# Eight-column expert masks spread by a matrix product in a fused scan, expert and feed-forward kernel

## The reference

```
tf    = sigmoid(sum(cond, -1))                      # one number for a batch
decay = exp(-exp(w)) * (0.5 + 0.5 * tf)             # channel x batch
a forward and a backward scan of exp(k) * v and of exp(k), with that decay
base  = sigmoid(r) * (num / den);  out = base * (0.8 + 0.2 * tf)
layer 0, experts:
gate  = argmax(x @ Wg.T);  p = softmax(x @ Wg.T)[gate]
h     = x @ A[e].T for all 8 experts, times one_hot(gate)
y     = sum over e of h[e] @ Bw[e].T, times 4 * p
layer 1, feed-forward:
w1, w2 made ternary (sign where |w| >= 0.7 * mean|w|);  gelu(x @ w1.T + b1) @ w2.T + b2
```

## Time and profile before

| | us |
|---|---|
| median of 3 runs | 103.11 |
| lowest and highest | 102.61, 103.37 |
| the profiled execution | 102.21 |
| its span on the core | 100.4 |

### The profile page before, as it was taken

How to read it: one execution, slowest core, us unless ns; L and a number is a source line. 1 busy time by engine, 2 the same in 40 slices (tenths; PEclk the granted TensorE clock), 3 DMA queues, 4 the chain that set the end, 5 groups by cost and what they waited for, 6 DMA issues and landing times. The chain is left out here.

```text
span 100.4 us, 2070 instructions
## 1 busy us (share of the span) xinstructions
PE 89.8 (89%) x633; PEld 80.9 (81%) x633; DVE 86.5 (86%) x203; ACT 79.9 (80%) x144; POOL 66.3 (66%) x90
## 2 busy tenths in 40 slices
PE   3897669989978999999799999999899999799980
PEld 2686549977777888888588888889799999699970
DVE  2479999999999999999999999999999997983330
ACT  4279999999986769999766589997997899976520
POOL 4067679979985697059769897999982967005310
PEclk9999999999999999999999999999999999999999
DMA  1889999700000000000000000000000021100005
GB/s 20 258 262 320 308 245 378 313 3 0 3 0 0 3 0 7 0 0 0 0 3 0 7 0 0 0 0 0 0 0 7 0 104 70 35 0 10 0 0 209
DMA packets 6886, 6.43 MB, mean 64 GB/s; under 512 B 2370, under 2 KB 6492, under 8 KB 6876
## 3 DMA queue, kind: packets, MB, share of 16 engines
q1 hardware_dynamic: 6868, 6.31, 20.1%
q10 hardware_dynamic: 8, 0.00, 0.0%
HBM read 5.26 MB, written 1.05 MB: 63 GB/s over the span
## 5 line engine op out<-in xcount | busy, mean ns | idle before, releaser
L298 POOL TENSOR_TENSOR h_lo<-h,h_hi 128x512 fp32r<-128x512 f32 x9 | 12.3, 1373 | 12.0 <-DVE h_hi L306 7.0
L794 DVE TENSOR_TENSOR_SCAN run<-bank,kv 128x256 f32<-128x256 f32 x32 | 20.0, 670 | 0.1
L1224 PE MATMUL bank<-xin_hi,w1T 128*128 128x256 f32 x64 | 15.8, 287 | 0.9 <-DVE xin_lo L292 0.5
L1156 PE MATMUL bank<-num,AT 128*128 128x256 f32 x64 | 15.5, 384 | 0.7 <-DVE hm L900 0.5
L1258 PE MATMUL bank<-w2T,h_hi 128*128 128x256 f32 x64 | 16.1, 288 | 0.0
L1258 PE MATMUL bank<-w2T,h_lo 128*128 128x256 f32 x64 | 15.6, 281 | 0.0
L611 ACT ACTIVATE h<-bank,bT 128x256 f32<-128x256 f32 x32 | 13.3, 478 | 2.8 <-PE bank L1224 2.6
L1224 PE MATMUL bank<-xin_lo,w1T 128*128 128x256 f32 x64 | 15.2, 278 | 0.0
L1172 PE MATMUL bank<-hm,BT 128*128 128x256 f32 x64 | 14.6, 382 | 0.1
L1224 PEld LDWEIGHTS bank<-xin_hi,w1T 128*128 128x128 f32 x64 | 12.0, 188 | 1.8 <-DVE xin_lo L292 0.8
L1156 PEld LDWEIGHTS bank<-num,AT 128*128 128x128 f32 x64 | 11.6, 190 | 2.2 <-issue 0.9
(11 more groups left out here) (141 smaller groups left out, 216.5 us busy)
## 6 DMA issues: line engine op xcount, KB each, us to landing
w_nat<-in_L_ffn_w_dram SPq DMA_DIRECT2D x2, 1024.0 KB, 8.3
F_nat<-in_fside_BxSxS_dram SPq DMA_DIRECT2D x4, 256.0 KB, 3.5
x_nat<-in_x_dram SPq DMA_DIRECT2D x4, 256.0 KB, 4.9
out_dram<-outb SPq DMA_DIRECT2D x3, 256.0 KB, 2.1
A_nat<-in_L_ffn_A_dram SPq DMA_DIRECT2D x1, 512.0 KB, 5.8
B_nat<-in_L_ffn_Bw_dram SPq DMA_DIRECT2D x2, 256.0 KB, 6.6
out_dram<-outb SPq DMA_DIRECT2D x2, 128.0 KB, 1.9
wv_rows<-in_L_cond_w_dram SPq DMA_DIRECT2D x2, 1.0 KB
```

Source lines behind the costliest of these rows:

```text
L298: eng.tensor_tensor(h_lo[:, b % 2, 2 * j:2 * j + 2], h32[:, b % 2, 2 * j:2 * j + 2], h_hi[:, b % 2, 2 * j:2 * j + 2].bitcast(F32), ALU.sub ...
L794: dve.tensor_tensor_scan(run[:, r, c, q], decay_ps[:, l, c, b:b + 1].broadcast_to([P, T]), kv[:, b, c, q], 0.0, ALU.mult, ALU.add).then_in ...
L1156: mm = pe.matmul(bank[H_BANK + k][:, (m % 2) * T:(m % 2 + 1) * T], AT[:, c, m * P:(m + 1) * P], num_at(0, b)[:, c], start=(c == 0), stop=( ...
L1224: mm = pe.matmul(bank[g_bank[g]][:, (f % 2) * T:(f % 2 + 1) * T], w1T[:, c, f * P:(f + 1) * P], part[:, b % 2, c], start=(c == 0 and part ...
```

## The change

The mask has 8 columns, one for each expert, instead of 128. `transpose_mask` turns it into 8 partitions, a new `copy_hot(b)` (ACT) takes these to SBUF, a new `spread_mask(b)` (PE) multiplies a constant 8x128 matrix `spread` (1 where p // 16 is e) with them, and `copy_mask(b)` takes the product as before. `spread` is made by POOL with a memset and two selects ahead of its first clip. The exponentials of `w` are taken on the four loaded rows, in place, before they are transposed, `decays` reads the transposed rows from PSUM, and `transpose_u`, which writes the same place, waits for both outputs of `decays`. The calls are moved in the lists as the diff shows: `decay_exps` stands ahead of the first key exponential; on PE `warm_up(2)` goes, four transposes of the identity (`fill(4)`) stand between `transpose_mask(0)` and `spread_mask(0)`, `place_residual(1)` and `spread_mask(1)` stand ahead of `expert_in(1, 0)`, `transpose_mask(2)` stands ahead of `expert_in(2, 1)` and `transpose_mask(3)` ahead of `hidden(0, 0)`; on DVE `select_expert(0, 0)` stands ahead of `gate(1)`. The second threshold is computed from the total itself instead of from the first. Three pairs of semaphores are merged, and the reciprocal of the mask has a call of its own.

```
         identb = sb("identb", [P, P], BF16)
-        expert_of = sb("expert_of", [P, P])
+        expert_of = sb("expert_of", [P, NE])
+        spread = sb("spread", [NE, P])
         recip_bias = sb("recip_bias", [P, 1])
...
         out_scale = sb("out_scale", [P, NB])
-        edecay = sb("edecay", [P, LAYERS * NC])
         eu = sb("eu", [P, LAYERS * NC])
...
         gsum = sb("gsum", [P, NI])
-        mask = sb("mask", [P, 2 * NT, P])
+        hot = sb("hot", [P, 2 * NT, NE])
+        hot_rows = sb("hot_rows", [NE, 2, T])
         mask_rows = sb("mask_rows", [P, 2, T])
...
         decay_ps, inv_gain_ps, scale_ps, cap_ps = [factor_columns(k * ND) for k in range(4)]
-        expert_ps = bank[DVE_BANK][:, EXPERT_AT:EXPERT_AT + P]
+        expert_ps = bank[DVE_BANK][:, EXPERT_AT:EXPERT_AT + NE]
         flat = "p a b -> p (a b)"
...
             if eng is nc.vector:
-                eng.wait_ge(inv_gain_psum, 1)
+                eng.wait_ge(inv_gain_ready, 2)
                 by = inv_gain_ps[:, l, :, b]
...
             for e in range(NE):
-                pool.memset(expert_of[:, e * P // NE:(e + 1) * P // NE], float(e)).then_inc(consts_ready, 1)
+                pool.memset(expert_of[:, e:e + 1], float(e)).then_inc(consts_ready, 1)
+
+            pool.memset(spread[:, :], 1.0).then_inc(consts_ready, 1)
+            pool.wait_ge(consts_ready, 5 + NE)
+            pool.affine_select(out=spread[:, :], in_=spread[:, :], compare_op=ALU.is_ge, fill=0.0, base=0,
+                               pattern=[[1, P]], channel_multiplier=-(P // NE)).then_inc(consts_ready, 1)
+            pool.wait_ge(consts_ready, 6 + NE)
+            pool.affine_select(out=spread[:, :], in_=spread[:, :], compare_op=ALU.is_ge, fill=0.0, base=P // NE - 1,
+                               pattern=[[-1, P]], channel_multiplier=P // NE).then_inc(consts_ready, 1)
...
-                pool.wait_ge(decay_ready, 1)
+                pool.wait_ge(decay_ready, 2)
                 pool.tensor_scalar(one_minus[:, :, :], decay[:, :, :], -1.0, 1.0, ALU.mult, ALU.add).then_inc(gain_steps, 1)
...
             def decay_exps():
-                act.wait_ge(front_psum, 2)
-                act.activation(edecay[:, :], bank[MISC_BANK][:, VEC_AT:VEC_AT + LAYERS * NC], ACT.Exp).then_inc(edecay_ready, 1)
+
+                act.wait_ge(wv_loaded, 16 * LAYERS)
+                act.activation(wv_rows[:, :], wv_rows[:, :], ACT.Exp).then_inc(edecay_ready, 1)
                 act.wait_ge(edecay_ready, 1)
-                act.activation(edecay[:, :], edecay[:, :], ACT.Exp, scale=-1.0).then_inc(edecay_ready, 1)
+                act.activation(wv_rows[:, :], wv_rows[:, :], ACT.Exp, scale=-1.0).then_inc(edecay_ready, 1)
...
+
+            def copy_hot(b):
+                act.wait_ge(hot_psum, b + 1)
+                act.activation(hot_rows[:, b % 2], bank[MISC_BANK][0:NE, MASK_AT:MASK_AT + T], ACT.Copy).then_inc(hot_copied, 1)
...
             cond_exp()
+            decay_exps()
             first_key_exp(0)
-            decay_exps()
             first_key_exp(1)
...
             sign_above(0)
+            copy_hot(0)
             copy_mask(0)
...
             keep_x1(0)
+            copy_hot(1)
             evacuate_wT(2)
...
             tanh(1)
+            copy_hot(2)
             evacuate_wT(4)
...
             act.preload_act_table_set("gelu_and_others")
+            copy_hot(3)
             gelus(0, 0)
...
                 dve.wait_ge(tf_ready, 3)
-                dve.wait_ge(edecay_ready, 2)
-                edecay_cols = edecay[:, :].rearrange("p (a b) -> p a b", b=1).broadcast_to([P, LAYERS * NC, NB])
+                dve.wait_ge(front_psum, 2)
+                edecay_cols = bank[MISC_BANK][:, VEC_AT:VEC_AT + LAYERS * NC].rearrange("p (a b) -> p a b", b=1).broadcast_to([P, LAYERS * NC, NB])
                 tf_cols = tf[:, 0:1, :].broadcast_to([P, LAYERS * NC, NB])
-                dve.tensor_tensor(bank[DVE_BANK][:, 0:ND].rearrange("p (a b) -> p a b", b=NB), edecay_cols, tf_cols, ALU.mult).then_inc(decay_psum, 1)
+                dve.tensor_tensor(bank[DVE_BANK][:, 0:ND].rearrange("p (a b) -> p a b", b=NB), edecay_cols, tf_cols, ALU.mult).then_inc(decay_ready, 1)
                 dve.tensor_tensor(decay[:, :, :], edecay_cols, tf_cols, ALU.mult).then_inc(decay_ready, 1)
...
                 dve.wait_ge(inv_gain_ready, 1)
-                dve.tensor_copy(bank[DVE_BANK][:, ND:2 * ND], inv_gain[:, :, :, :].rearrange(flat4)).then_inc(inv_gain_psum, 1)
+                dve.tensor_copy(bank[DVE_BANK][:, ND:2 * ND], inv_gain[:, :, :, :].rearrange(flat4)).then_inc(inv_gain_ready, 1)
...
                 r, u = ring(l, b)
-                dve.wait_ge(decay_psum, 1)
+                dve.wait_ge(decay_ready, 1)
                 if q == DEN:
...
-            def expert_mask(b):
-
+            def gate_reciprocal(b):
                 both = slice(NT * b, NT * (b + 1))
...
+
+            def expert_mask(b):
+
...
                 if b >= 2:
-                    dve.wait_ge(mask_psum, b - 1)
+                    dve.wait_ge(hot_psum, b - 1)
                 for i in range(NT * b, NT * (b + 1)):
-                    dve.tensor_scalar(mask[:, i % (2 * NT)], expert_ps, bank[DVE_BANK][:, IDX_AT + i:IDX_AT + i + 1],
+                    dve.tensor_scalar(hot[:, i % (2 * NT)], expert_ps, bank[DVE_BANK][:, IDX_AT + i:IDX_AT + i + 1],
                                       bank[DVE_BANK][:, GREC_AT + i:GREC_AT + i + 1], ALU.is_equal, ALU.mult).then_inc(mask_ready, 1)
...
                 dve.tensor_scalar(thr[:, 0], bank[WT_BANK][:, 0:2], 1.0 / (DFF * C), 0.7, ALU.mult, ALU.mult).then_inc(thr_ready, 1)
-                dve.wait_ge(thr_ready, 1)
-                dve.tensor_scalar(thr[:, 1], thr[:, 0], -1.0, None, ALU.mult).then_inc(thr_ready, 1)
+                dve.tensor_scalar(thr[:, 1], bank[WT_BANK][:, 0:2], 1.0 / (DFF * C), -0.7, ALU.mult, ALU.mult).then_inc(thr_ready, 1)
...
             den_times_rec(0, 1)
+            gate_reciprocal(0)
             expert_mask(0)
...
             select_expert(0, 1)
+            select_expert(0, 0)
             gate(1)
-            select_expert(0, 0)
             add_den(0, 2)
...
             forward(0, 3, NUM)
+            gate_reciprocal(1)
             expert_mask(1)
...
             den_times_rec(0, 3)
+            gate_reciprocal(2)
             expert_mask(2)
...
             forward(1, 1, NUM)
+            gate_reciprocal(3)
             expert_mask(3)
...
+            def fill(n):
+
+                pe.wait_ge(thr_ready, 2)
+                for _ in range(n):
+                    pe.transpose(bank[WT_BANK][:, 0:P], ident[:, :], ident[:, :])
+
...
             def transpose_w():
-                pe.wait_ge(wv_loaded, 16 * LAYERS)
+                pe.wait_ge(edecay_ready, 2)
                 pe.transpose(bank[MISC_BANK][:, VEC_AT:VEC_AT + LAYERS * NC], wv_rows[:, :], ident[0:LAYERS * NC, 0:LAYERS * NC]).then_inc(front_psum, 1)
...
                 pe.wait_ge(uv_loaded, 16 * LAYERS)
-                pe.wait_ge(edecay_ready, 1)
+                pe.wait_ge(decay_ready, 2)
                 pe.transpose(bank[MISC_BANK][:, VEC_AT:VEC_AT + LAYERS * NC], uv_rows[:, :], ident[0:LAYERS * NC, 0:LAYERS * NC]).then_inc(front_psum, 1)
...
                     pe.wait_ge(vs_ready, F_read(NB - 1))
-                    pe.wait_ge(BT_ready, 2)
+                    if k:
+                        pe.wait_ge(BT_ready, 2)
                 else:
...
                 for n in range(NT):
-                    mm = pe.transpose(bank[MISC_BANK][:, MASK_AT + n * P:MASK_AT + (n + 1) * P], mask[:, NT * (b % 2) + n], ident[:, :])
-                mm.then_inc(mask_psum, 1)
+                    mm = pe.transpose(bank[MISC_BANK][0:NE, MASK_AT + n * P:MASK_AT + (n + 1) * P], hot[:, NT * (b % 2) + n], ident[:, :])
+                mm.then_inc(hot_psum, 1)
+
+            def spread_mask(b):
+                pe.wait_ge(hot_copied, b + 1)
+                pe.wait_ge(consts_ready, 7 + NE)
+                pe.matmul(bank[MISC_BANK][:, MASK_AT:MASK_AT + T], spread[:, :], hot_rows[:, b % 2], start=True, stop=True).then_inc(mask_psum, 1)
...
 
             warm_up(4)
             spread_cond()
-            warm_up(2)
             transpose_first_F(0)
             transpose_w()
             transpose_first_F(1)
...
             place_residual(0)
             expert_in(0, 0)
             transpose_mask(0)
+            fill(4)
+            spread_mask(0)
             transpose_weights(0)
             gate_logits(1)
             transpose_weights(1)
...
             expert_out(0)
             transpose_weights(2)
             transpose_mask(1)
+            place_residual(1)
+            spread_mask(1)
             expert_in(1, 0)
-            place_residual(1)
             transpose_weights(3)
             gate_logits(2)
             expert_out(1)
             expert_in(2, 0)
             transpose_weights(4)
+            transpose_mask(2)
             expert_in(2, 1)
```

(5 more changed lines are left out.)

69 lines of the change are left out of this document (43 added, 26 removed).

## The result

The changed kernel takes 107.62 us (median of 4 runs, 105.84 to 109.46) against 103.22 us (4 runs of before beside them, 102.61 to 103.37). I forecast 104.6 and a range up to 105.3. The direction and the place were right; the size was not.

What follows compares the result with a forecast made beforehand. DVE was taken to set the pace to about 70 us, PE as second bound. The 2.3 us on offer were lost to the masks' longer way: 102.21 plus 1.5 gives 103.7, plus 0.9 for the median 104.6; range 102.3 to 105.3.

Steps and rivals of the forecast that it cites:

- The front, 0.2 carried: Beginning, up to the scans: earlier decays let the second chunk gain 0.2 us, bounds 0 to 0.35.
- The compare, 0.66 to 0.17: Mask compares on DVE: 8 columns instead of 128 save 0.5 us four times, 2.0 us in all (1.6 to 2.1).
- The rival that kept the whole 0.66: Mask compares: 8 columns still take 0.66 us if PSUM scalars set the length; 105 us, sharing the forecast's 0.50.
- The first mask, 0.4 left and PE 0.25 late: First mask: copied mask at 29.3, 0.4 of 0.8 us saving left; PE reaches expert_in(1, 1) at 30.75, against 30.5.
- PE's cost of a spread, 0.6: Each mask's spread product holds PE for 0.45 to 0.8 us, taken as 0.6.
- The second mask decides, DVE 0.5 behind (0.3 to 0.7): Second mask: residual and spread delay expert_in(1, 0), DVE's second product starts at 39.9 or later, saving gone, 0.5 us behind.
- The third mask, still 0.5: Third mask: copied mask comes at 49.8 to 50.4, so DVE stays 0.5 us behind (0.15 to 0.75).
- The fourth mask: PE stands 1.5 to 2 us for the mask; hidden(0, 0) starts at 61.2, hidden(0, 2) at 64.1, 2.3 late.
- The end, 1.5 late: End of the kernel: after ACT's 0.55 us of slack, 1.5 us late, 102.21 becomes 103.7.
- My chain from there on: From hidden(0, 2): gelus 2.1 late, log_den(1, 2) and gelus(1, 0) 1.5 late, rigid from 72.48 to the end.
- The clock falls, 0.08: Rival: the stop at 59 us or missing dummies slow PE's clock, another 1.5 us, 106 us; chance 0.08.
- The two rows that I took for a slower pace: Clock rival's evidence: two transposes took 0.64 us at 4.00, where four of the second group were loaded in 0.57.

Runs made afterwards that it cites:

- k12: Kernel before with only the new way of the decays and both thresholds read from PSUM: 102.62 us median, ratio 0.999.
- k10: Changed kernel with warm_up(2) back and 14 dummy transposes in idle places: 105.22 us at the full clock, 107.17 us median, ratio 1.045.
- e8: Kernel before with compares of 8 of the 128 columns, no spread, right masking left out: 102.05 us median, ratio 0.994.
- e5: Changed kernel with place_residual(1) behind expert_in(1, 0) again, the spread still ahead of it: 106.43 us median, ratio 1.038.
- e7: Kernel before with only transpose_mask(3) moved ahead of hidden(0, 0): 105.03 us median, 103.19 in its one execution at the full clock.
- k11: k10 with the fourth mask's transposes and spread behind hidden(0, 1), both its copies between the first two gelus: 104.33 us at the full clock, ratio 1.030.
- k16: k10 with the spread's matrix and copied rows padded to 128 partitions, 120 of them zero: 104.38 us at clock 1.00, median 105.08, ratio 1.022.
- k17: k11's order of the fourth mask plus k16's spread over 128 partitions: 103.67, 103.70 and 104.07 us at the full clock, median 103.89, ratio 1.012.
- e1: Changed kernel with its two dummy transposes ahead of the first F transposes put back: 107.0 us median.
- e2: Kernel before without its two dummy transposes ahead of the first F transposes: 104.33 us median, 101.94 in one execution at clock 0.997.
- e4: Kernel before with only the new way of the decays, second threshold still computed from the first: 104.59 us median, ratio 1.017.
- k19: k17 with ACT's first copy of each mask made twice: 104.43, 104.50, 104.91 and 105.50 us at the full clock.

## Why the prediction was right or wrong

The steps in turn, at the full clock unless said otherwise:

- *The front, 0.2 carried*: 0.1 at most (k12). The scan did start 0.39 early (5.30) in the changed kernel, but the second scan, whose keys stand behind `transpose_w`, started only at 6.37 and ended 0.09 early; by the first compare nothing was left, 26.15 in k10 against 26.14. POOL's three constants took 0.9 us (k10, from 1.9 to 2.8), not 1.2, and were hidden as I said.
- *The compare, 0.66 to 0.17*: this term was mis-sized. The pair holds DVE 0.41, so 0.25 is saved each time and 1.0 in all, under my lower bound of 1.6; e8 measures 0.95. I took the maxima as the nearest row, though they lack the two PSUM scalars. The rival that kept the whole 0.66 was as far off. Of the 0.66 us only 0.25 went with 240 columns, some 1 ns each; most of the length isn't in the columns. Whether it is in the scalars no run shows.
- *The first mask, 0.4 left and PE 0.25 late*: wrong on both. ACT's first copy began at 28.17 in k10 and not 27.90, the copied mask was there at 29.7 and not 29.3, and DVE's product began at 29.80 after a wait, 0.06 behind before's: the saving was gone one mask earlier than I said. PE reached `expert_in(1, 1)` at 31.12 against 30.52, 0.6 late.
- *PE's cost of a spread, 0.6*: nearly right. From the spread's product to the next one it is 0.63 with 8 rows and 0.48 with 128; padding gave back 0.84 for four, so the price for the kernel is about 0.7 each (0.48 and 0.21).
- *The second mask decides, DVE 0.5 behind (0.3 to 0.7)*: right in kind, down to which product would wait and for whom, `expert_in(1, 0)`. The size was 1.0 in k10, 1.64 in the profiled execution with its fall. PE's list brought the 0.6 us of the first mask along (`keep_x1(0)` at 36.61 against 36.01), where I had carried 0.25. What e5 showed is that I blamed the wrong neighbour besides: not the residual, but the copy that waits behind `keep_x1` in ACT's list, and the spread.
- *The third mask, still 0.5*: 1.4. DVE's compare gained its 0.25 (1.2 behind ahead of it, 0.95 after it), then DVE waited 0.37 for the mask. `transpose_mask(2)`, moved ahead of `expert_in(2, 1)`, made PE stand 0.50 for the compare, and the spread came behind `expert_in(2, 1)` with gaps of 0.33 on both sides.
- *The fourth mask*: `hidden(0, 0)` behind a stand of 1.5 to 2 us; it was 2.30. Stall and order were right, and e7 and k11 price the order at 1.0 us.
- *The end, 1.5 late*: 3.0 (k10). `hidden(0, 2)` began at 65.48, where I had 64.1: 0.9 of the 1.4 is the compare that came later than I said (61.69, not 60.8), the rest its length and the spread. My chain from there on held: 3.66 late became 3.02 through the slack of ACT. By single effects: before 102.04; narrow compare -0.95; four spread products 1.7 (taken as what the second four cost); four first copies 0.8 (likewise); the gaps 0.84 (k16); the fourth mask's order 0.9 (k11). The sum is 105.3, against 105.22 measured. So close a match is partly luck: the last two gave only 1.5 together (k17), and each term rests on one or a few executions.
- *The clock falls, 0.08*: far too little. All four executions of the changed kernel had a fall. At 0.984 it took 105.84 and 106.40, 0.6 to 1.2 over k10 at the full clock; at 0.952 some 3.9 over it. That is the rest of the distance to the median. In its profiled execution the fall came at 15.7 us, long before the stop at 59, and e1 and e2 clear the dummies. But the stop can have a part: in e5 PE resumed at 61.89 behind a stop of 2.31 us and the clock fell after 63 us, in k16 it resumed at 61.80 behind 2.41 and the clock fell after 62 us; with a stop of 2.30 or 2.31 it did not fall in the profiled executions of k10, the changed kernel and e1. The price of a fall also varied: in e5 the stretch from the fourth compare to the end of the span is 43.3 us against 41.8 in k10, 1.5 us more. The two rows that I took for a slower pace don't compare: 0.64 is of two products and 0.57 of the loads of four, whose products took 0.60 at 38.21 in before.

The step that failed was thus the price of a mask. It saved DVE 0.25 us and not 0.5, and its longer way made PE 0.6 us late at the first mask and not 0.25, and DVE 1.4 behind at the third and not 0.5. The 0.9 us that DVE was later than I said at the fourth compare, and some 0.5 that the compare and the spread behind it took beyond my figures, make the 3.0 at the end instead of 1.5. What stays open: what brings a fall on, why the changed kernel had one in all its four executions, and of some three times the length (by the mean clock) in two of them. And no version here beats before by more than the measurement can tell, apart from e8, which leaves the masking out; k12 equals it.

## What to carry to other kernels

Where an engine has no idle time in a stretch, price what an edit adds to it at full length, with the gaps around it, before you price what it saves elsewhere, and carry a delay of the first stage into all later ones. The length of a short instruction hardly followed its columns here: take its row from one with the same operands, not from the smallest instruction near it. A product with few rows of weights between full ones can be cheaper padded with zeros, as it was here, and an instruction that waits goes behind those that are ready.

## What the runs showed of the hardware

- A product with 8 rows of weights leaves PE's loads without issue for 0.33 us afterwards, and also before it where it follows full loads directly (k10, 49.85); with 128 rows, 120 of them zero, the gap behind it is gone and the kernel gains 0.84 us (k16). The Trainium skill (TensorEngine Tiling (Array Packing), Key Properties) says that a change of tiling mode drains TensorE. For few rows the traces agree. For the transposes with 8 columns they show no such gap: in k10 those at 47.80 took 0.09 us and the full loads behind them began at 47.92.
- A DVE instruction of 128x2 from SBUF to SBUF took 1.17 us beside a POOL product of 1.28 that had begun 0.13 earlier (e4); another in e7 took 1.29. In before, where it began 0.07 ahead of POOL's product, it took 0.17. Read from PSUM the second threshold took 0.15 in every trace that has it so. The Trainium skill (SBUF — State Buffer, SBUF: two separate sides) calls the port pair of these two engines an exclusive lock held for the whole instruction; these traces agree. Whether this is also what the eight full-clock executions of before at 103.2 to 103.8 had was not settled; it can't be all, since k10 and k19 have such executions too (106.40 and 105.50) and read the threshold from PSUM.
- The mean granted clock was 0.983 or lower in 30 of 53 executions of before itself. Where a profile shows such a fall, it is from 2.4 to 1.2 GHz, and lasted 3.4 us in the ten profiles in which the clock came back. Before at 0.983 took 0.4 us or more over its lower group at the full clock. In ten of the eleven profiled executions with a fall PE had stood idle for part of the few us ahead of it (busy 0.19 of 1 us at 12 in the changed kernel, nothing at 60 in e5 and k16), but the same idle stretches are in profiles without a fall (0.09 of 1 us at 12 in before, nothing at 61 in k10), so they don't decide it alone. In the eleventh, of e8, PE had been busy throughout from 3 to 9 us; the clock then stayed at the lower level from about 9.5 us to the end, and it took 148.9 us:

```profile
PEclk9985555555555555555555555555555555555555
```
